# VectorE adds the negated maxima for four of sixteen score units of a self pair, in place of the fourth product

## What is computed

```python
h = _layernorm(x, ln1_g, ln1_b)
x = _attention(h, h, sa_wq, sa_wk, sa_wv, sa_wo, sa_bo) + x
h = _layernorm(x, ln2_g, ln2_b)
x = _attention(h, cond_emb, ca_wq, ca_wk, ca_wv, ca_wo, ca_bo) + x
h = _layernorm(x, ln3_g, ln3_b)
p = h @ ff_w1 + ff_b1
a, gate = (p[..., :D_FF], p[..., D_FF:])
h = a * jax.nn.gelu(gate, approximate=False) @ ff_w2 + ff_b2
return h + x
```

## Time and profile before

| | us |
|---|---|
| median of 3 runs | 1226.41 |
| lowest and highest run | 1225.41, 1226.55 |
| span of the profiled execution | 1223.4 |
| TensorE busy | 1188.0 |
| VectorE busy | 767.6 |
| GpSimd busy | 743.3 |
| ScalarE busy | 642.8 |

### The profile page before, as it was taken

How to read it: one execution, slowest core, us unless ns; L and a number is a source line. 1 busy time by engine, 2 the same in 40 slices (tenths; PEclk the granted TensorE clock), 3 DMA queues, 4 the chain that set the end, 5 groups by cost and what they waited for, 6 DMA issues and landing times. The chain is left out here.

```text
span 1223.4 us, 23620 instructions
## 1 busy us (share of the span) xinstructions
PE 1188.0 (97%) x9385; PEld 783.6 (64%) x9385; DVE 767.6 (63%) x1289; ACT 642.8 (53%) x954; POOL 743.3 (61%) x381
## 2 busy tenths in 40 slices
PE   3899999999999999999999999999999999999998
PEld 3655665666566656666655664666666666678887
DVE  4757566566565576675665766368677877675433
ACT  3448554445445446744544454557755586536332
POOL 1196787886876976877877868865556436321000
PEclk9899999999999999999999999999999999999999
DMA  3010000000000000000000000011111110010000
GB/s 111 14 27 10 6 22 12 5 11 23 6 10 23 6 10 23 6 10 14 15 10 12 10 13 6 23 31 49 50 39 32 32 32 18 9 38 18 18 18 18
DMA packets 63540, 25.76 MB, mean 21 GB/s; under 512 B 34552, under 2 KB 61384, under 8 KB 63432
## 3 DMA queue, kind: packets, MB, share of 16 engines
q1 hardware_dynamic: 63375, 24.25, 7.5%
q10 hardware_dynamic: 56, 0.01, 0.0%
HBM read 21.62 MB, written 2.10 MB: 19 GB/s over the span
## 5 line engine op out<-in xcount | busy, mean ns | idle before, releaser
L1403 POOL TENSOR_TENSOR acc<-acc,probs 128x1024 f32<-128x1024 f32 x192 | 458.9, 2390 | 64.5 <-ACT probs L1274 52.7
L1274 ACT ACTIVATE probs<-psum 128x1024 f32<-128x1024 f32 (+1 forms) x320 | 317.1, 1030 | 276.1 <-PE psum L845 271.0
L1048 DVE TENSOR_REDUCE m_part<-psum 128x2 f32<-128x1024 f32 x256 | 308.9, 1222 | 223.9 <-PE psum L822 223.9
L859 PE MATMUL psum<-probs,val 128*64 128x512 f32 x1024 | 244.9, 603 | 0.0
L1403 POOL TENSOR_TENSOR acc<-probs 128x1024 f32<-128x1024 f32 (+1 forms) x64 | 153.0, 2391 | 149.0 <-ACT probs L1274 142.3
L1085 DVE SCALAR_TENSOR_TENSOR xr<-psum,d_cols,xr 128x256 f32<-128x256 f32 x512 | 207.8, 475 | 34.5 <-PE psum L882 33.9
L859 PEld LDWEIGHTS psum<-probs,val 128*64 128x64 f32 x1024 | 63.3, 136 | 113.9 <-issue 99.0
L845 PE MATMUL psum<-row_max,minus 64*128 64x512 f32 (+1 forms) x640 | 126.5, 389 | 0.0
L845 PE MATMUL psum<-q_hi,k_hi 64*128 64x512 f32 x512 | 101.7, 393 | 0.3 <-DVE m_part L1048 0.3
L845 PE MATMUL psum<-q_lo,k_hi 64*128 64x512 f32 x512 | 100.9, 390 | 0.0
L845 PE MATMUL psum<-q_hi,k_lo 64*128 64x512 f32 x512 | 100.8, 389 | 0.0
(11 more groups left out here) (147 smaller groups left out, 2162.1 us busy)
## 6 DMA issues: line engine op xcount, KB each, us to landing
xr<-in_x SPq DMA_DIRECT2D x8, 256.0 KB, 5.0
wv_raw<-in_L_xattn_sa_wv SPq DMA_DIRECT2D x8, 256.0 KB, 2.9
wqk_raw<-in_L_xattn_sa_wq SPq DMA_DIRECT2D x16, 128.0 KB, 2.5
wqk_raw<-in_L_xattn_sa_wk SPq DMA_DIRECT2D x16, 128.0 KB, 2.4
wo_raw<-in_L_xattn_sa_wo SPq DMA_DIRECT2D x16, 128.0 KB, 2.4
d_cols<-d_rows SPq DMA_DIRECT2D x128, 2.0 KB, 2.1
wqk_raw<-in_L_xattn_ca_wq SPq DMA_DIRECT2D x16, 128.0 KB, 2.5
probs<-in_L_xattn_ff_w SPq DMA_DIRECT2D x8, 256.0 KB, 3.3
```

What stands on the lines that cost most here:

```text
L859: mm = pe.matmul(psum[d, PVB + half, :], values(J)[0:plan.ks, kt, own], probs[buffer_of(J, u)][0:plan.ks, h, :], start=(kt == 0), stop=(kt ...
L1048: dve.tensor_reduce(m_part[:, half, :, t, kh], psum[:, bank0:bank0 + 2, :], AX.X, ALU.max).then_inc(s_x_read, 1)
L1274: act.activation(probs[buffer_of(J, u)][0:plan.ks, :, :], psum[0:plan.ks, bank0:bank0 + 2, :], ACT.Exp, scale=SCALE).then_inc(s_exp, 1)
L1403: pool.tensor_tensor(total, last if kt == 1 else total, now, ALU.add).then_inc(s_acc, 1)
```

## The change

The constant `TAKEN_BY_VECTOR` names four units of a self pair: 2, 6, 9 and 13. In them TensorE makes three products and not four, and a new step `take` on VectorE ("U" in the orders) adds the negated maxima to the unit, from PSUM into its buffer of `probs`. ScalarE takes the exponential of these in place, in SBUF. So the unit's buffer in PSUM is free when VectorE has read it, and the exponential waits for VectorE.

For that add the maxima of a half have to stand on all partitions. `m_cols` is now reduced negated, `move_m` writes it to a tensor in DRAM with one DMA, and a new step `spread_m` ("N" in the orders) reads it back to all 128 partitions of `less_max[a]`, 4 KB each. `less_max` has one buffer for each half, so `spread_m` waits until the units of the pair before have been read. The fourth product of the other twelve units, and of the cross pairs, reads rows 0 and 64 of the same tensors, with a matrix `one_row` of +1 in place of `minus`. The two `row_max` tensors and the clearing of them go away.

```diff
+TAKEN_BY_VECTOR = (2, 6, 9, 13)
+
+
+def on_vector(J, u):
+
+    return J < NSELF and u in TAKEN_BY_VECTOR
+
+
+def taken(J, u):
+
+    return min(J, NSELF) * len(TAKEN_BY_VECTOR) + sum(v < u for v in TAKEN_BY_VECTOR if J < NSELF)
...
-MOVED = before(lambda p: 16 * 2)
+MOVED = before(lambda p: 16 if p.own else 32)
...
-    "sp": "G++@-58.84 O@9.97 T-@10.13 W++@12.95 M1@38.05 M0+@40.90",
+    "sp": "G@-163.98 W@-97.39 M0@-2.58 N0@7.33 O@9.71 M1@11.75 N1@19.41 T@61.16",
...
-        top = [sb(f"row_max{b}", [P, SEQ], F32R) for b in range(2)]
-        minus = sb("minus", [P, P], F32R)
+        less_max = [sb(f"less_max{a}", [P, 2, HALF], F32R) for a in range(2)]
+        one_row = sb("one_row", [P, P], F32R)
...
+        top = [t[:].rearrange("p h n -> p (h n)") for t in less_max]
+        max_rows = nc.dram_tensor("less_max_rows", (2, 2, HALF), F32, kind="Internal").ap()
...
-                if J < 2:
-                    sp.wait_ge(s_fill, FILLS)
-                if J >= 2:
-                    sp.wait_ge(s_s, U0[J - 1])
-                n = 4 if own else 8
+                if own:
+                    after(sp, s_less_max[a], 16 * J)
+                else:
+                    sp.wait_ge(s_s, U0[J if J == NSELF else J - 1])
+                    sp.wait_ge(s_taken, taken(J, 0))
+                if own:
+                    sp.dma_start(max_rows[a].rearrange("h (p t) -> p h t", p=P),
+                                 m_cols[a][:].bitcast(F32).rearrange("p (h t) -> p h t", h=2)).then_inc(s_m[a], 16)
+                    return
                 for h in range(2):
-                    row, q0 = h * DH, a * HALF
-                    cols = m_cols[a] if own else c_cols[J % 2]
-                    sp.dma_start(top[J % 2][row:row + 1, q0:q0 + n * P].bitcast(F32).rearrange("o (p t) -> o p t", p=P),
-                                 cols[:, n * h:n * (h + 1)].bitcast(F32)).then_inc(s_m[a], 16)
+                    sp.dma_start(top[J % 2][h * DH:h * DH + 1, :].bitcast(F32).rearrange("o (p t) -> o p t", p=P),
+                                 c_cols[J % 2][:, 8 * h:8 * (h + 1)].bitcast(F32)).then_inc(s_m[a], 16)
...
+            def spread_m(J, a):
+                sp.wait_ge(s_m[a], MOVED[J + 1])
+                if J:
+                    sp.wait_ge(s_s, U0[J - 1] + 8 * (a + 1))
+                    sp.wait_ge(s_taken, taken(J - 1, 8 * (a + 1)))
+                sp.dma_start(less_max[a][:].bitcast(F32), max_rows[a].partition_broadcast(P)).then_inc(s_less_max[a], 16)
...
-                    pe.wait_ge(s_m[half if plan is SELF else 0], MOVED[J + 1])
+                    if plan is CROSS:
+                        pe.wait_ge(s_m[0], MOVED[J + 1])
+                if plan is SELF and not on_vector(J, u):
+                    pe.wait_ge(s_less_max[half], 16 * (J + 1))
                 ks = slice(kt * plan.ks, (kt + 1) * plan.ks)
                 qs = slice(half * HALF, (half + 1) * HALF)
                 wait_buffer(pe, ("S", J, u))
-                for i, (w, x) in enumerate(((k_hi, q_hi), (k_hi, q_lo), (k_lo, q_hi), (minus, top[J % 2]))):
+                last = 2 if on_vector(J, u) else 3
+                for i, (w, x) in enumerate(((k_hi, q_hi), (k_hi, q_lo), (k_lo, q_hi))):
                     for h in range(2):
-                        mm = pe.matmul(psum[0:plan.ks, bank_of(("S", J, u), h), :], w[rows_of(h), ks if i < 3 else slice(0, plan.ks)], x[rows_of(h), qs], start=(i == 0), stop=(i == 3))
+                        mm = pe.matmul(psum[0:plan.ks, bank_of(("S", J, u), h), :], w[rows_of(h), ks], x[rows_of(h), qs], start=(i == 0), stop=(i == last))
+                if last == 3:
+                    for h in range(2):
+                        x = less_max[half][rows_of(h), h, :] if plan is SELF else top[J % 2][rows_of(h), qs]
+                        mm = pe.matmul(psum[0:plan.ks, bank_of(("S", J, u), h), :], one_row[rows_of(h), 0:plan.ks], x, start=False, stop=True)
...
-                                      AX.X, ALU.max).then_inc(s_x_read, 1)
+                                      AX.X, ALU.max, negate=True).then_inc(s_x_read, 1)
...
-                                  AX.X, ALU.max).then_inc(s_m_cols, 1)
+                                  AX.X, ALU.max, negate=True).then_inc(s_m_cols, 1)
...
+            def take(J, u):
+                half = u // SELF.kt
+                bank0 = bank_of(("S", J, u))
+                back = user_before(J, u)
+                dve.wait_ge(s_less_max[half], 16 * (J + 1))
+                if back:
+                    dve.wait_ge(s_pv, U0[back[0]] + back[1] + 1)
+                    dve.wait_ge(s_acc, added(*back))
+                if J == 0 and u == 7:
+                    dve.wait_ge(s_c_hi, KC)
+                dve.wait_ge(s_s, U0[J] + u + 1)
+                dve.tensor_tensor(probs[buffer_of(J, u)][:], psum[:, bank0:bank0 + 2, :], less_max[half][:].bitcast(F32), ALU.add).then_inc(s_taken, 1)
...
+                p = probs[buffer_of(J, u)][0:plan.ks, :, :]
+                if on_vector(J, u):
+                    act.wait_ge(s_taken, taken(J, u) + 1)
+                    act.activation(p, p, ACT.Exp, scale=SCALE).then_inc(s_exp, 1)
+                    return
...
-                for b in range(2):
-                    pool.memset(top[b][:].bitcast(F32), 0.0).then_inc(s_fill, 1)
-                pool.memset(minus[:].bitcast(F32), 0.0).then_inc(s_minus_zero, 1)
-                pool.wait_ge(s_minus_zero, 1)
+                pool.memset(one_row[:].bitcast(F32), 0.0).then_inc(s_row_zero, 1)
+                pool.wait_ge(s_row_zero, 1)
                 for r in (slice(0, 1), slice(DH, DH + 1)):
-                    pool.memset(minus[r, :].bitcast(F32), -1.0).then_inc(s_fill, 1)
+                    pool.memset(one_row[r, :].bitcast(F32), 1.0).then_inc(s_fill, 1)
```

## The result

| | before | after |
|---|---|---|
| median of the runs | 1226.48 us (1225.41 to 1226.63) | 1241.93 us (1241.49 to 1243.94) |
| profiled span | 1223.4 us | 1240.1 us |
| mean granted clock of TensorE | 0.997 | 0.991 |

The changed kernel is slower: ratio 1.0134, 95% interval 1.0121 to 1.0146. The forecast was 1217.3 us, in a range from 1208 to 1230; both are missed.

A forecast was written before the change was run, and what follows sets the result against it. TensorE was taken to set the pace. From the 1223.4 us span, -9.0 (pairs), +1.7 (first spread), -4.3 (opening) and +2.5 (turn) gave 1214.3; 3.0 more for the median made 1217.3 us, range 1208 to 1230.

The forecast's parts named there:

- What bounds the kernel, and the price of a product: Self pairs: TensorE sets the pace; a unit's fourth product costs it about 0.228 us, 0.91 us a pair.
- the ceiling: Most that removing four fourth products in each of 16 pairs can save TensorE: 14.6 us.
- The add: VectorE's new add per taken unit: 1.18 us, or 1.13 us queued behind another operation; 4.5 us a pair.
- The carried pair: One self pair worked through in the new orders: VectorE takes back 0.35 of 0.91 us, 9.0 us gained over 16 pairs.
- The exponentials: ScalarE's exponentials of taken units come 1 to 1.5 us later; costed at nothing.
- GpSimd's sums: GpSimd's adds, which queue behind the later exponentials of taken units; costed at nothing.
- The spread (rival 3): Broadcast of maxima lands late, TensorE stops at every pair's first unit; at 6.5 us landing 21 us, so 1238; chance 0.15.
- VectorE takes it all (rival 2): VectorE's adds in its full stretch eat TensorE's saving; pair stays 47.15 us, total 1226.3 us; chance 0.22.
- The opening: Start of the kernel, context load moved forward: first K product at about 19.4 instead of 23.69, -4.3 us.
- the wait for the first spread: First pair's first unit waits for its maxima to reach all partitions: +1.7 us, once, between 0.5 and 2.1.
- The turn: From self to cross pairs: 2 MB of weight loads ahead of the last self pair's sums, +2.5 us, between 0 and 4.

The follow-up runs named there:

- item 2: Three kernels on w1_late: no unit taken (1235.87 us); that with the four fourth products left out (1226.27 us); fourth products and adds both kept (1241.54 us).
- w1_late: Changed kernel with three of four pairs of first-layer weight loads moved behind the last self pair's sums: 1234.66 us, 1.0069 of the kernel before.
- left_out: none_taken with the fourth product of units 2, 6, 9 and 13 left out and nothing in its place: 1226.27 us, 1.0004 of the kernel before.
- quiet3: quiet0 with units 12, 14 and 15 taken in thirteen self pairs: 1236.39 us, 1.0088 of the kernel before.
- quiet_mid: quiet0 with units 12, 13 and 14 taken in thirteen self pairs: 1223.06 us, 0.9980 of the kernel before.
- item 6: Five kernels on the old order, taking other units than the change does, to test the place of the adds: 1220.16 to 1241.08 us.
- none_taken: w1_late with no unit taken, all fourth products kept, exponentials of units 6 and 13 a little earlier: 1235.87 us, 1.0076 of the kernel before.
- quiet4b: quiet0 with units 1, 12, 14 and 15 taken in twelve self pairs: 1241.08 us, 1.0127 of the kernel before.
- w1_early_in_before: Kernel before with all four pairs of first-layer weight loads put ahead of the last self pair's sums in SyncE's queue: 1237.76 us, ratio 1.0101.
- quiet0: old_order_way with the context load second and the first pair's second-half maxima reduced, stored and spread earlier: 1226.01 us, 1.0004 of the kernel before.
- old_order_way: Kernel before with its orders and all fourth products, no adds, but maxima sent by DRAM to all partitions: 1231.07 us, ratio 1.0048.

## Why the prediction was wrong

**What bounds the kernel, and the price of a product.** Right. A taken unit lasts 0.70 us where 0.69 was said, and the busy time of 100.7 us was rightly not used: leaving the products out gave 7.5 us in fifteen pairs, below even the 13.7 of the ceiling.

**The add.** Right: 1.22 us, and 1.13 where the next operation is queued behind it (639.83 to 640.96).

**The carried pair (-9.0 us).** This is the step that failed. The places were right: the second projection group waits for the maximum ahead of it (640.06). But the carrying charged the new order only at the places named and took the rest of it as free, which no row of the kernel before could show. The order itself costs 0.25 us in an ordinary pair (0.30 with the way over DRAM) and 1.6 us in each of the two with a normalisation, with nothing taken. The waits that were carried were also too small: 0.35 of the 0.91 us were to come back, and 0.69 do, 0.37 of them even without an add (0.23 at the projection group, most of the rest at the spread, item 2) and 0.32 behind the adds. So the exchange gains 0.22 us a pair instead of 0.56, and the order takes more than that. For 1 to 16, read one kernel after another: +0.5 the way, +7.9 the new order, -7.5 the products, +4.4 the adds, and 0.3 between w1_late and the kernel after; sum +5.6. Forecast was -8.4.

**The exponentials.** "I cost that at nothing" held for the units of this change: left_out to w1_late has no place where TensorE waits for an exponential for more than 0.1 us in the pair looked at. Elsewhere it would not have held: quiet3's pair is 0.9 us longer from just this. GpSimd's sums, costed at nothing in the same sentence, cost quiet_mid 0.7 us in two pairs (item 6).

**The spread (rival 3).** The sum of 6.2 us from the maxima's end to the landing was near the best case. In the first halves of the kernel after it is 5.8 to 8.0: the store lands after 1.5 to 3.2 us (2.0 was taken), the spread after 3.8 to 5.9 (4.0 was taken). The point from which it decides, 6.2 + 1.1 = 7.3 us, was right: the pairs that wait have 7.4 to 8.0, those that don't 6.1 to 7.0, except pair 10, which follows a long pair and has 7.8 (pair 0, in the opening, waits at 5.8). So the rival is true in some pairs, and its price is 2.6 us in w1_late, not the 21 of its working, since the excess is some tenths and not in every pair.

**VectorE takes it all (rival 2)** comes near the length of the pair (47.15 said, 47.26 measured), but in part by luck: the adds take 0.3 us, and the order, of which it says nothing, takes 0.3 with the way over DRAM.

**The opening.** Right. The first K product was put at 19.4 and came at 19.89; with the wait for the first spread (forecast 1.7, row 1.45) the first unit is 2.20 us earlier, forecast 2.6:

```profile
46.73 0.49 PE L848 MATMUL psum<-q_hi,k_hi 64*128 64x512 f32 x2 [1.45 <-DMA less_max<-less_max_rows]
```

**The turn (+2.5, between 0 and 4).** The reciprocal was put about 3 us later relative to the last self pair and came 3.0 later. The term was mis-sized, 8.1 us, because it was counted as a wait only. The waits themselves were 3.8 us, inside the range; the stop then took TensorE's clock from 1.00 to 0.50 for the following 10 us, in which sixteen value products took 7.09 us, 0.44 each, where twelve of the last self pair took 2.79 before the stop, 0.23 each.

**What the sum left out.** One wait of 1.1 us stands at pair 16's first unit, for its maxima (none in none_taken or in the kernel before); it lies in the stretch 1 to 16. And 5.35 us from pair 17 on. The tables for the cross pairs are new too, and the prediction did not speak of them. The kernels with the old tables need 35.9 and 364.1 to 364.9 us there (but for quiet4b's 366.46 and w1_early_in_before's 37.01), those with the new ones 37.4 to 40.7 and 366.7 to 367.6, whatever they take. In left_out, whose clock does not fall there, pair 18 takes 19.85 us where quiet0 has 18.27, pair 26 (both hold a normalisation) 19.08 against 18.28, and pair 24 17.00 against 16.38. Which of the new places costs them was not tried.

The range was too narrow for the same reason: each bound was drawn from the terms that were written down, and the moved work between them had none.

## What to carry to other kernels

Where a diff replaces whole tables of order, price the order first, as a change of its own: a kernel with the new order and the old work tells in one run what the idea is charged with. Before work moves to another engine, ask for each moved piece which buffer it gives back late, and what stands behind it in the queue of the engine that comes next; idle time of the engine that takes the work answers neither. A load that is early for its own use can stand ahead of a small transfer that the bound engine needs now, and a stop of TensorE can cost its clock on top.

## What the runs showed of the hardware that was not expected

- A stop costs more than itself: 5.2 us of waiting made 16 to 17 longer by 11.6 us, with 0.50 of the clock through the 10 us behind it; 3.8 us of waiting made it longer by 8.1; 2.4 us of waiting in old_order_way were followed by 5 us at 0.66. With the same idle time of about 1.4 us, the stretch from 843 to 857 ran at 0.83 and 0.68 in one kernel and at 1.00 in another, and one and the same kernel differs from run to run (w1_late: mean clock 0.994 in the profiled run, 0.996 and 0.997 in the others). So a short stop may or may not be charged.
- 512 KB read by 128 partitions from the same 4 KB landed after 3.9 to 4.3 us in the median, like an ordinary load of that size (4.0). Its neighbours land late instead: weight loads of 128 KB issued beside it landed after 3.7 to 4.7 us in the kernel after, and after 2.3 to 2.5 apart from it.
- The store of 4 KB from 128 partitions to DRAM took 1.5 to 3.2 us in the kernel after (median 2.0), and up to 2.6 in quiet0, where no weight load stands behind it. But quiet_mid, with the same orders of SyncE, has stores of 3.3 and 3.5 us, so the loads behind it are not its only cause.
- The same four normalisations on VectorE took 4.32 us beside GpSimd's work and 1.38 without.
